# Eight loads ahead of a barrier, and four ScalarE operations made two, in a GRU, experts, state-space and attention kernel

## The chip, the cores and the metric

One core of a Trainium2 chip runs the whole program. The metric is the device time of one execution, in microseconds. PE is the matrix engine (TensorE), PEld its weight loads, DVE the vector engine, ACT the scalar engine, POOL GpSimd, SP the engine that issues the DMAs. PE's granted clock has two levels, 1.2 and 2.4 GHz; a PEclk of 0.5 is the lower and 1.0 the higher.

## The reference, cut to what matters

Four layers act on 4 x 1024 tokens of 128 features, each on the layer-normalised input and each added to the residual: two gated recurrences, eight experts of which each token takes one, a state-space layer with a small network, and a local attention of depth 2. The change touches the seam between the second and third, and one step of the third:

```
yf = einsum('te,etd->td', onehot(top1, E), y_all)          # experts; x = x + yf

u, z  = split(einsum('bld,ed->ble', rmsnorm(x), in_proj_w))
u     = silu(conv(u))
dbc   = einsum('bld,ed->ble', u, x_proj_w)
dt, Bm, Cm = split(dbc, [8, 8 + 16])
dt    = softplus(einsum('blr,dr->bld', dt, dt_proj_w) + dt_proj_b)
s     = s * exp(dt * A) + (dt * u) * Bm                    # 16 states, scanned over time
```

## The kernel before

The token matrix `x` lies transposed in SBUF, features on partitions and the 4096 tokens along the row, and is worked on in eight chunks of 512 tokens (`CH`). Beside it stand `branch`, of the same size, and the constants; both live for the whole program. Each stage is a block with one hand-written program for each engine, and semaphores order the engines. A block ends with a barrier of all engines: each engine drains, POOL gathers them and lets them go; then POOL clears the stage's semaphores, and a second barrier follows.

**Experts** (`experts`, line 514). Tokens are scattered to DRAM by expert, worked on in 40 blocks of 128, and POOL scatters each block's result rows with an indirect DMA into `from_experts` in DRAM (line 739), four to a group. At the end both SP (line 600) and POOL (lines 745, 746) wait for the last of these scatters, `stored[0]` and `stored[1]`. `branch` was written by the recurrences and is not read any more once they are through; the experts do not use it.

**Norm** (`return_and_norm`, line 212). In a new block SP loads the result rows back, a chunk of 256 KB at a time (line 242), into a ring of four buffers `rows`, each again when PE has transposed what was in it (`back`). Behind these eight loads in SP's queue stand eleven loads of the next stage's weights (line 245). PE transposes a chunk (line 259), DVE adds it to `x` (line 303), PE centres it (line 267), ACT squares, PE takes the mean (line 272), ACT computes the two roots (lines 288 to 295), and DVE writes the normalised chunk to `branch` and the root-mean-square one to `x0` (lines 308, 309).

**Time step** (`mamba_and_attention`, line 935). After the convolution come eight chunks `t`, in four blocks of two (`k` = 0, 1). For each block PE computes `dbc` for both chunks (line 1093) into `bank[k]`: rows 0 to 31 are B and C, rows 32 to 39 the low-rank time step, rows 64 to 127 repeat B and C. ACT copies rows 32 to 63 with a bias that makes row 40 a one (line 1240, `dt_low`), then rows 0 to 31 (line 1243, into `rest`), which SP stores to DRAM (line 1029), then all rows as bf16 (line 1244, `parts`), whose lower parts DVE works out (lines 1395 to 1403). PE computes the raw time steps (line 1101) into two banks for a chunk. ACT takes absolute value (line 1251, one for each bank), exponential (line 1254) and logarithm (line 1256), DVE completes the softplus (line 1409). A `matmul` here is issued as two records, so a chunk has four at line 1093 and four at line 1101.

**Scan and attention.** SP broadcasts the stored rows to `b_all` (line 1044), POOL multiplies (line 1348), and 128 steps of the scan follow, with the attention behind them, for the rest of the program. `dt_low` lies in `b_all[32:64, 1:3]`, buffers that the second and third broadcast fill.

## Time and profile before

| | us |
|---|---|
| median of three timed runs (1602.8 to 1604.7) | 1603.2 |
| the profiled execution | 1607.0 |
| its span, from the first to the last instruction | 1605.2 |
| PE, DVE, ACT, POOL busy in the span | 1343, 1208, 1026, 914 |
| from POOL's last scatter of results (its start) to PE's first transpose | 12.2 |
| the norm, from that transpose to DVE's last product | 30.4 |
| ACT's first copy of the time-step stage to POOL's first product of the scan | 43.1 |

The profile is of one execution, so durations and starts are read from it, and a time is compared with the median of the runs. Busy shares are averages over stages with different limits; for a change in one stage the order of time there is read, with what each engine waited for.

### The profile page before, as it was taken

Reading aid. Unit: us, or ns where it says so; the run is one execution under the profiler, and the core shown is the slowest. Engines: PE = TensorE matmul, PEld = TensorE weight load, DVE = VectorE, ACT = ScalarE, POOL = GpSimd, SP = SyncE. Lnnn points to the kernel's source line nnn. Section 1 sums busy time; section 2 is a strip of 40 time slices with the busy share of each in tenths; the row PEclk is TensorE's granted clock in tenths of the full one; section 3 lists DMA queues with packets and bytes.
Section 4 is the critical chain, followed back from the end, with each engine's and each line's share of the span. In section 5 each row is a group of like instructions: output and inputs, shape, how many; then the busy total and the mean of one; then the engine's idle time right before and its main releaser. Section 6 shows DMA issues by size and latency. Waiting matters only on the chain.

```text
span 1605.2 us, 23619 instructions
## 1 busy us (share of the span) xinstructions
PE 1343.4 (84%) x8058; PEld 722.2 (45%) x8058; DVE 1208.1 (75%) x1788; ACT 1025.7 (64%) x1718; POOL 913.9 (57%) x476
## 2 busy tenths in 40 slices
PE   6748199477677888898888889999999999999987
PEld 2315188322223333333333355555555555555552
DVE  2984255267788999999998588888888888888862
ACT  4424055378744554555553588888888888888863
POOL 0343434100298899899895466565555566656540
PEclk9877599787689999999999899999999999999999
DMA  3201221300334433336442112121211111111100
GB/s 114 79 1 32 65 57 48 93 10 7 67 99 100 99 105 92 101 106 170 119 146 63 35 26 47 28 47 28 47 28 43 31 40 34 47 41 34 34 21 27
DMA packets 71038, 96.77 MB, mean 60 GB/s; under 512 B 13651, under 2 KB 32390, under 8 KB 70662
## 3 DMA queue, kind: packets, MB, share of 16 engines
q1 hardware_dynamic: 68614, 90.51, 21.8%
q0 software_dynamic: 2304, 4.74, 0.9%
q8 instruction: 65, 1.06, 0.3%
q14 instruction: 55, 0.45, 0.1%
HBM read 63.73 MB, written 8.41 MB: 45 GB/s over the span
## 4 chain that ended last, share of the span: by engine, by line
PE 46%; ACT 12%; DVE 12%; issue 7%; POOL 2%; DMA 0%; DVEq 0%; SPq 0%; ACTq 0%; POOLq 0%
PE at_two L1766 6%; DVE ssm_state L1445 6%; PE glu_bank L1702 5%; PE ssm_bank L1129 4%; PE at_one L1862 4%; DVE ssm_seen L1454 4%; ACT home_dt L1971 4%; PE glu_bank L1683 4%; PE at_two L1744 3%; PE at_two L1796 3%; PE at_one L1774 3%; PE glu_bank L1728 2%; PE ssm_bank L1163 2%; POOL ssm_dbu L1348 1%; PE ssm_bank L1126 1%
## 5 line engine op out<-in xcount | busy, mean ns | idle before, releaser
L1348 POOL TENSOR_TENSOR ssm_dbu<-ssm_dtu,ssm_b_all 128x1024 f32<-128x1024 f32 x128 | 297.5, 2357 | 31.5 <-DVE home_dt L1409 31.5
L1981 POOL TENSOR_TENSOR at_direct<-at_direct,home_u 128x1024 f32<-128x1024 f32 x64 | 150.9, 2358 | 276.1 <-DVE home_u L2072 276.1
L1274 ACT ACTIVATE ssm_bank<-home_dt,ssm_decay 128x512 f32<-128x512 f32 x256 | 174.6, 690 | 153.1 <-DVE ssm_state L1445 151.7
L1129 PE MATMUL ssm_bank<-ssm_seen,ident 128*128 128x512 f32 x512 | 250.6, 614 | 25.2 <-DVE ssm_seen L1454 23.0
L1129 PEld LDWEIGHTS ssm_bank<-ssm_seen,ident 128*128 128x128 f32 x512 | 97.7, 196 | 146.0 <-issue 86.9
L1445 DVE TENSOR_TENSOR_SCAN ssm_state<-ssm_bank,ssm_carry,ssm_dbu 128x512 f32<-128x512 f32 x128 | 155.8, 1268 | 9.4 <-ACT ssm_bank L1274 9.4
L1445 DVE TENSOR_TENSOR_SCAN ssm_state<-ssm_bank,ssm_dbu 128x512 f32<-128x512 f32 x128 | 147.9, 1206 | 15.3 <-ACT ssm_bank L1274 7.8
L1766 PE MATMUL at_two<-home_u,at_hs 128*128 128x512 f32 x256 | 126.2, 616 | 7.6 <-ACT at_kT L1909 5.5
L1986 POOL TENSOR_TENSOR home_z<-home_z,at_inv 128x1024 f32<-128x1024 f32 x64 | 121.4, 1897 | 18.6 <-DVE at_inv L2083 18.6
L2109 DVE TENSOR_REDUCE at_peak<-at_scores 128x8 f32<-128x1024 f32 x64 | 78.2, 1223 | 61.9 <-PE at_scores L1829 50.6
L1992 POOL TENSOR_TENSOR at_direct<-at_direct,at_rnorm 128x1024 f32<-128x1024 f32 x64 | 121.8, 1903 | 0.2
L1358 POOL TENSOR_TENSOR ssm_seen<-ssm_state,ssm_c_all 128x1024 f32<-128x1024 f32 x40 | 94.1, 2353 | 40.2 <-PE ssm_bank L1129 25.3
L1454 DVE TENSOR_TENSOR ssm_seen<-ssm_state,ssm_bank 128x1024 f32<-128x1024 f32 x88 | 105.5, 1199 | 8.7 <-issue 8.2
L1971 ACT ACTIVATE home_dt<-at_two 128x1024 f32<-128x1024 f32 x64 | 65.4, 1022 | 69.9 <-PE at_two L1796 69.9
L1702 PE MATMUL glu_bank<-home_z 128*128 128x512 f32 (+1 forms) x192 | 91.6, 600 | 1.6 <-DVE home_z L2102 1.2
L2072 DVE TENSOR_TENSOR home_u<-home_dt 128x256 f32<-128x256 f32 x256 | 91.1, 418 | 0.0
L2049 DVE TENSOR_REDUCE at_sums<-home_u 128x16 f32<-128x1024 f32 x64 | 77.4, 1209 | 7.3 <-ACT home_u L1888 7.3
L2079 DVE TENSOR_REDUCE at_total<-home_z 128x8 f32<-128x1024 f32 x64 | 77.6, 1213 | 6.9 <-ACT home_z L1918 6.9
L2065 DVE TENSOR_TENSOR at_direct<-home_dt 128x512 f32<-128x512 f32 x128 | 82.3, 684 | 0.0
L1766 PEld LDWEIGHTS at_two<-home_u,at_hs 128*128 128x128 f32 x256 | 46.6, 193 | 75.3 <-issue 48.9
L2116 DVE TENSOR_TENSOR home_z<-at_scores,at_peak 128x1024 f32<-128x1024 f32 x64 | 78.4, 1224 | 2.2
L1796 PEld LDWEIGHTS at_two<-ident,home_z 128*128 128x128 f32 x512 | 58.4, 140 | 47.5 <-issue 47.5
(247 smaller groups left out, 3100.2 us busy)
## 6 DMA issues: line engine op xcount, KB each, us to landing
ssm_b_all<-ssm_b_rows SPq DMA_DIRECT2D x128, 256.0 KB, 3.4
at_v_mix<-at_v SPq DMA_DIRECT2D x112, 128.0 KB, 2.3
ssm_c_all<-ssm_b_rows SPq DMA_DIRECT2D x40, 256.0 KB, 3.7
at_hs<-branch SPq DMA_DIRECT2D x64, 128.0 KB, 2.4
moe_w<-in_moe_w SPq DMA_DIRECT2D x16, 256.0 KB, 6.0
moe_slot_rows<-moe_to_experts SPq DMA_DIRECT2D x40, 64.5 KB
x<-in_x SPq DMA_DIRECT2D x8, 256.0 KB, 3.7
ssm_norm_rows<-moe_from_experts SPq DMA_DIRECT2D x8, 256.0 KB, 3.2
```

Source lines behind the costliest of these rows:

```text
L1129: last = nc.tensor.matmul(bank[Y0 + half][:], ident[:], seen[:, n % 2, half], start=False, stop=n == STATES - 1)
L1274: nc.scalar.activation(bank[DA0 + half][:], chunk_of(dt[:, half], t), ACT.Exp, scale=decay[:, half, n:n + 1]).then_inc(r[f"da{half}"], 1)
L1348: nc.gpsimd.tensor_tensor(dbu[:, i % RING], dtu[:, t % 2], b_all[:, i % B_RING:i % B_RING + 1, :].broadcast_to([P, 2, CH]), ALU.mult).then ...
L1445: nc.vector.tensor_tensor_scan(state[:, i % RING, half], bank[DA0 + half][:], dbu[:, i % RING, half], start, ALU.mult, ALU.add).then_inc(r ...
L1454: nc.vector.tensor_tensor(seen[:, j % 2], state[:, j % RING], bank[C0][:].unsqueeze(1).broadcast_to([P, 2, CH]), ALU.mult).then_inc(r["see ...
L1702: return nc.tensor.matmul(glu[to][0:size, :], w1[:, c // LAYER_CHUNKS, m * HID + first:m * HID + first + size], normed, start=True, stop=True)
L1766: last = nc.tensor.matmul(two[:, half], at, wqkv[g // PER_LAYER][:, half * INNER:(half + 1) * INNER], start=True, stop=True)
L1796: last = nc.tensor.transpose(two[:, h // 4, (h % 4) * TILE:(h % 4 + 1) * TILE], prob[m % 2][:, h], ident[:])
L1971: nc.scalar.activation(pT[:].rearrange("p h j -> p (h j)"), two[:].rearrange("p a n -> p (a n)"), ACT.Copy).then_inc(s["pT_copied"], 1)
L1981: nc.gpsimd.tensor_tensor(direct[:, n % TURNED], direct[:, n % TURNED], crossed[n % 2], ALU.add).then_inc(s["added"], 1)
L1986: nc.gpsimd.tensor_tensor(prob[m % 2], prob[m % 2], inv[:, m % 2].unsqueeze(2).broadcast_to([P, HEADS, TILE]), ALU.mult).then_inc(s["weigh ...
L1992: nc.gpsimd.tensor_tensor(heads, heads, rnorm[:, n % 2].unsqueeze(2).broadcast_to([P, 2 * HEADS, HEAD]), ALU.mult).then_inc(s["scaled"], 1)
```

## The change

1. `return_and_norm` no longer loads the result rows. SP issues all eight loads at the end of its program in `experts`, right behind its wait for the scatters, and each has a semaphore of its own, `returned[0]` to `returned[7]`, which lives for the whole program. They go into `branch`, chunk by chunk (`returned_rows`), and PE transposes from there. The ring `rows` is gone.
2. POOL's last two waits for the scatters are gone.
3. `dt_low` and the rows of B and C are one copy of rows 0 to 63 into `low`, with a bias of 64 rows (`unit`); SP stores rows 0 to 31 of it. It waits for the store of two chunks before. SP waits for all stores before its second broadcast.
4. The pairs of PSUM banks are one tensor each (`pair`), and the two absolute values of a chunk are one over 1024 elements.

```diff
+def returned_rows(mem, t):
+    return mem["branch"][:, t * CH:(t + 1) * CH].rearrange("p (j d) -> p j d", d=P)
...
 def return_and_norm(...):
-        rows = sb("rows", [P, RING, CH // P, P])
...
         def _(sp):
-            for t in range(CHUNKS_IN):
-                if t >= RING:
-                    sp.wait_ge(back, t - RING + 1)
-                    sp.wait_ge(returned[t % RING], 16 * (t // RING))
-                sp.dma_start(rows[:, t % RING], results[t * CH:(t + 1) * CH].rearrange("(j p) d -> p j d", p=P)
-                             ).then_inc(returned[t % RING], 16)
             for to, of in loads:
                 sp.dma_start(to, of).then_inc(loaded, 16)
             sp.wait_ge(loaded, 16 * len(loads))
-            for n in returned:
-                sp.wait_ge(n, 16 * (CHUNKS_IN // RING))
...
-                    pe.wait_ge(returned[t % RING], 16 * (t // RING + 1))
+                    pe.wait_ge(returned[t], 16)
...
 def experts(...):
             for n in range(2):
                 sp.wait_ge(stored[n], 16 * GROUP * PAIRS)
+            for t in range(2 * SEQS):
+                sp.dma_start(returned_rows(mem, t), from_experts[t * CH:(t + 1) * CH].rearrange("(j p) d -> p j d", p=P)
+                             ).then_inc(mem["returned"][t], 16)
...
                     pool.sem_inc(s["emptied"], 1)
-            for n in range(2):
-                pool.wait_ge(stored[n], 16 * GROUP * PAIRS)
...
 def mamba_and_attention(...):
-        dt_low = b_all[32:64, 1:3]
+        low = b_all[0:64, 1:3]
-        bank = [ring.enter_context(nc.psum_tensor(f"ssm_bank{n}", [P, CH], F32)) for n in range(8)]
+        pair = [ring.enter_context(nc.psum_tensor(f"ssm_bank{n}", [P, 2, CH], F32)) for n in range(4)]
+        bank = [pair[n // 2][:, n % 2] for n in range(8)]
...
-                sp.wait_ge(s["b_low"], done(t))
-                sp.dma_start(b_rows[:, t * CH:(t + 1) * CH], rest[0:2 * STATES, t % 2]).then_inc(b_stored[t % 2], 16)
+                sp.wait_ge(s["low"], done(t))
+                sp.dma_start(b_rows[:, t * CH:(t + 1) * CH], low[0:2 * STATES, t % 2]).then_inc(b_stored[t % 2], 16)
...
                     if i == 1:
                         sp.wait_ge(s["dtraw"], done(2 * SEQS - 1))
+                        for m in b_stored:
+                            sp.wait_ge(m, 16 * (1 + SEQS))
...
-                    pe.wait_ge(s["dt_low"], done(t))
+                    pe.wait_ge(s["low"], done(t))
...
-                                                dt_low[:, k][0:9], start=True, stop=True)
+                                                low[32:41, k], start=True, stop=True)
...
                     act.wait_ge(s["dtraw"], freed(t))
-                    nc.scalar.activation(dt_low[:, k], bank[k][32:64, :], ACT.Identity, bias=unit[32:64]
-                                         ).then_inc(s["dt_low"], 1)
                     act.wait_ge(b_stored[k], b * 16 + 16)
-                    nc.scalar.activation(rest[0:2 * STATES, k], bank[k][0:2 * STATES, :], ACT.Copy).then_inc(s["b_low"], 1)
+                    nc.scalar.activation(low[:, k], bank[k][0:64, :], ACT.Identity, bias=unit[:]).then_inc(s["low"], 1)
...
-                    for half in range(2):
-                        last = nc.scalar.activation(size[:, k, half], bank[2 + 2 * k + half][:], ACT.Abs)
-                    last.then_inc(s["size"], 1)
+                    nc.scalar.activation(size[:, k], pair[1 + k][:], ACT.Abs).then_inc(s["size"], 1)
```

SP at the seam between experts and norm; the exit of the experts' block is line 518 (513 after), the norm's block begins with the branch that waits for `release`. Before:

```order
L597 DMA moe_slot_rows<-moe_to_experts 128x129
L518 UNCONDITIONAL_BRANCH [waits moe_stored1,moe_stored0]
L236 UNCONDITIONAL_BRANCH [waits barrier_Pool_Activation_PE_DVE_SP_release]
L242 DMA ssm_norm_rows<-moe_from_experts 128x4x128 x4
L242 DMA ssm_norm_rows<-moe_from_experts 128x4x128 [waits gru_norm_arrived1,gru_norm_moved]
```

and after:

```order
L591 DMA moe_slot_rows<-moe_to_experts 128x129
L596 DMA branch<-moe_from_experts 128x4x128 [waits moe_stored1,moe_stored0]
L596 DMA branch<-moe_from_experts 128x4x128 x7
L513 UNCONDITIONAL_BRANCH
L239 UNCONDITIONAL_BRANCH [waits barrier_Pool_Activation_PE_DVE_SP_release]
L242 DMA home_dt<-in_in_w 128x512
```

The eight loads moved from behind the barriers to ahead of them, and the weights' loads are now the first behind them.

POOL at the same place; `gather` is its wait for the other engines, the ISA rows are clears of semaphores. Before:

```order
L739 DMA moe_from_experts<-moe_out_rows,moe_owners 9216x128 x3
L518 UNCONDITIONAL_BRANCH [waits moe_stored0,moe_stored1]
L518 ISA [waits barrier_Pool_Activation_PE_DVE_SP_gather]
L218 ISA [waits barrier_Pool_Activation_PE_DVE_SP_gather]
L218 ISA
```

and after:

```order
L736 DMA moe_from_experts<-moe_out_rows,moe_owners 9216x128 x3
L513 UNCONDITIONAL_BRANCH [waits moe_stored0]
L513 ISA [waits barrier_Pool_Activation_PE_DVE_SP_gather]
L223 ISA [waits barrier_Pool_Activation_PE_DVE_SP_gather]
```

The wait for `stored1`, which the last four scatters raise, is gone (the one left is for the group before), and one clear less stands at the norm's exit; one more stands at the end of the program.

ACT in a block of two chunks of the time step, before (the names in the waits are those of semaphores freed by earlier stages):

```order
L1240 ACTIVATE ssm_b_all<-ssm_bank,ssm_unit 32x512 [waits gru_gated_0,gru_fed_0]
L1243 ACTIVATE ssm_dtu<-ssm_bank 32x512 [waits ssm_b_stored0]
L1244 ACTIVATE ssm_parts<-ssm_bank 128x512
L1240 ACTIVATE ssm_b_all<-ssm_bank,ssm_unit 32x512 [waits gru_gated_0,gru_fed_0]
L1243 ACTIVATE ssm_dtu<-ssm_bank 32x512 [waits ssm_b_stored1]
L1244 ACTIVATE ssm_parts<-ssm_bank 128x512
L1251 ACTIVATE ssm_seen<-ssm_bank 128x512 [waits gru_x_done,gru_gated_0]
L1251 ACTIVATE ssm_seen<-ssm_bank 128x512
L1254 ACTIVATE ssm_seen<-ssm_seen 128x1024 [waits gru_gated_1]
L1256 ACTIVATE ssm_seen<-ssm_seen 128x1024 [waits gru_h_0]
```

and after:

```order
L1239 ACTIVATE ssm_b_all<-ssm_bank,ssm_unit 64x512 [waits ssm_b_stored0,gru_off_1,gru_fed_0]
L1240 ACTIVATE ssm_parts<-ssm_bank 128x512
L1239 ACTIVATE ssm_b_all<-ssm_bank,ssm_unit 64x512 [waits ssm_b_stored1,gru_off_1,gru_fed_0]
L1240 ACTIVATE ssm_parts<-ssm_bank 128x512
L1246 ACTIVATE ssm_seen<-ssm_bank 128x1024 [waits gru_h_1,gru_off_1]
L1248 ACTIVATE ssm_seen<-ssm_seen 128x1024 [waits gru_gated_0]
L1250 ACTIVATE ssm_seen<-ssm_seen 128x1024 [waits gru_gated_1]
```

Two instructions a chunk are gone, and the wait for the store stands ahead of the copy that PE's matmuls need.

## Rows read from the trace of the kernel before

**Rows 1.** The page's first row, and the chain that ended last, by engine.
```profile
span 1605.2 us, 23619 instructions
...
PE 46%; ACT 12%; DVE 12%; issue 7%; POOL 2%; DMA 0%; DVEq 0%; SPq 0%; ACTq 0%; POOLq 0%
```

**Rows 2.** Waits of SP, 255 to 345 us: total, times, longest.
```profile
SPq L518 <- PEq L518: 6.1, 1, 6.1
```

**Rows 3.** Line 518: op xcount, ns min/median/max, first and last start.
```profile
L518 POOLq DRAIN  x2: 128/3035/5942, 293.5 to 299.6; - x2
...
L518 PEldq DRAIN  x1: 1187/1187/1187, 284.5 to 284.5; - x1
...
L518 POOLq EVENT_SEMAPHORE_RANGE_CLEAR  x1: 305/305/305, 299.8 to 299.8; - x1
```

**Rows 4.** Timeline, 284 to 304 us: start, length, engine, line, [idle <- releaser].
```profile
284.51 1.16 PE L676 MATMUL moe_bank<-moe_w_now,moe_hidden 128*128 128x128 f32 x8 [0.34 <-ACT moe_hidden L719]
...
291.01 0.96 POOL L739 DMA_INDIRECT moe_from_experts<-moe_out_rows,moe_owners  x1 [0.30 <-issue]
...
300.42 2.04 SPq L242 DMA_DIRECT2D ssm_norm_rows<-moe_from_experts  x4
...
303.22 1.97 PE L259 MATMUL ssm_norm_bank<-ident,ssm_norm_rows 128*128 128x128 f32 x8 [17.55 <-DMA ssm_norm_rows<-moe_from_experts]
```

**Rows 5.** Loads: ssm_norm_rows to landing; SP's timeline; window (us, busy, PEclk, DMA).
```profile
DMA to landing us min/median/max: 2.8/3.2/4.6
...
33.48 11.73 SPq L346 DMA_DIRECT2D moe_w<-in_moe_w  x16
...
304.00:307.00 3.00, 3.00 (x9) 1.53 (x8) 1.38 (x2) 0.00 (x0) 0.00 (x0) 0.50 0.81 238
```

**Rows 6.** Line 1029, the stores of ssm_b_rows.
```profile
DMA to landing us min/median/max: 1.6/1.6/1.6
```

**Rows 7.** Timeline of ACT, 384 to 428 us.
```profile
385.01 0.59 ACT L1243 ACTIVATE ssm_dtu<-ssm_bank 32x512 f32<-32x512 f32 x1
385.50 0.57 ACT L1244 ACTIVATE ssm_parts<-ssm_bank 128x512 bf16<-128x512 f32 x1
386.92 0.68 ACT L1240 ACTIVATE ssm_b_all<-ssm_bank,ssm_unit 32x512 f32<-32x512 f32 x1 [0.85 <-PE ssm_bank L1093]
...
388.83 1.08 ACT L1251 ACTIVATE ssm_seen<-ssm_bank 128x512 f32<-128x512 f32 x2
389.95 1.06 ACT L1254 ACTIVATE ssm_seen<-ssm_seen 128x1024 f32<-128x1024 f32 x1
...
397.53 0.68 ACT L1240 ACTIVATE ssm_b_all<-ssm_bank,ssm_unit 32x512 f32<-32x512 f32 x1 [0.49 <-PE ssm_bank L1093]
...
409.35 1.05 ACT L1251 ACTIVATE ssm_seen<-ssm_bank 128x512 f32<-128x512 f32 x2
```

**Rows 8.** PE, 380 to 428 us: timeline, then groups of instructions.
```profile
401.05 3.70 PE L1093 MATMUL ssm_bank<-home_u,ssm_dbc_w 128*128 128x512 f32 x8
406.61 4.18 PE L1101 MATMUL ssm_bank<-ssm_b_all,ssm_dt_w 9*128 9x512 f32 x8 [1.86 <-ACT ssm_b_all L1240]
410.71 6.65 PE L1093 MATMUL ssm_bank<-home_u,ssm_dbc_w 128*128 128x512 f32 x8
417.29 4.46 PE L1101 MATMUL ssm_bank<-ssm_b_all,ssm_dt_w 9*128 9x512 f32 x8
...
L1093 PE MATMUL ssm_bank<-home_u,ssm_dbc_w 128*128 128x512 f32 x32 | 22.8, 878 | 9.6 <-issue 9.6
L1101 PE MATMUL ssm_bank<-ssm_b_all,ssm_dt_w 9*128 9x512 f32 x32 | 17.0, 675 | 1.9 <-ACT ssm_b_all L1240 1.9
```

**Rows 9.** Windows of the time-step stage: busy time (x), PEclk, DMA share, GB/s.
```profile
380.00:427.00 47.00, 39.38 (x64) 14.52 (x64) 28.11 (x48) 40.67 (x58) 2.35 (x1) 0.72 0.14 31
...
395.30:405.90 10.60, 9.45 (x20) 3.43 (x19) 7.03 (x13) 9.77 (x15) 0.55 (x1) 0.96 0.05 13
```

**Rows 10.** Timeline of POOL, 286 to 428 us.
```profile
427.37 2.35 POOL L1348 TENSOR_TENSOR ssm_dbu<-ssm_dtu,ssm_b_all 128x1024 f32<-128x1024 f32 x1 [31.52 <-DVE home_dt L1409]
```

15 lines of the change are left out of this document (7 added, 8 removed).

## The prediction

> **What bounds the kernel now.** The profiled execution spans 1605.2 us, and its time is 1607.0 us, 1.8 us more for what lies around the span; the median of the timed runs is 1603.2 us. All differences below are made on the profiled execution and taken from the median. I read first the chain that ended last [rows 1]: nearly half of it is PE, and most of the rest ACT and DVE. But the scan and the attention, from POOL's first product at 427.4 [rows 10] to the end, are not touched by the change. So the question is by how much two serial stretches ahead of them, both of them on the way of everything behind, become shorter, and whether the rest simply starts that much earlier.
>
> Next I read what SP waits for at the end of the experts [rows 2], then the exit of that block instruction by instruction [rows 3], then the order of time around it [rows 4]. The reader is to see a gap with no work in it. POOL's last scatter of result rows starts at 291.01 and its record ends 0.96 us later, at 291.97. SP has seen the last scatter landed at 293.3, since it then waits 6.1 us at the exit [rows 2] until 299.6. What holds all engines is POOL: its drain at the block's exit starts at 293.5 and takes 5.94 us [rows 3]. SP's first load starts at 300.42, and PE's first transpose at 303.22 [rows 4]. Last come the eight chunks of the time-step stage (384.3 to 427.4) on ACT and PE [rows 7 to 9].
>
> **Part 1, the loads ahead of the barrier.** Removed: PE's wait for the first load, 303.22 - 300.42 = 2.80 us [rows 4]. The eight loads now lie in SP's program right behind its wait for the scatters, and start at 293.3. The first four took 2.04 us to issue [rows 4], 0.51 each, so eight take 4.1 us and SP is at the exit at 297.4. The nearest row against that is the stretch of 16 loads of the same size issued back to back, 11.73 us or 0.73 each [rows 5], by which SP arrives at 293.3 + 5.9 = 299.2. Both are ahead of 299.4, where POOL's drain ends today. So the issue costs nothing as long as POOL's drain covers it; uncovered it would cost 4.1 to 5.9 us.
>
> The first load lands 2.8 us after its issue [rows 5], at 296.1, before PE is there. The loads moved 238 GB/s at their densest [rows 5], so the 2.1 MB take 8.8 us; with 1.7 us ahead of the first data (2.8 less the 1.1 that one chunk takes at that rate) they are in by 303.8, while PE takes the chunks over some 20 us. No transpose waits.
>
> **Part 2, POOL's two waits removed.** POOL no longer waits for the last scatters before it drains, so it gets there at 291.97 instead of 293.49, 1.52 us sooner. Whether the drain's end moves too depends on what the 5.94 us are, and the trace leaves two readings. On PE the drain of the same exit starts at 284.5, takes 1.19 us, and ends when the last matmuls do (284.51 + 1.16) [rows 3, 4]: a drain there is what the engine has left to do. If POOL's is left-over work of the scatters too, its end at 299.4 stays, and the gain is 0. If the drain itself sets the work off, it ends at 291.97 + 5.94 = 297.9, and the gain is 1.52 us, provided that SP is there. What speaks for the second: scatters follow one another with 0.30 us between them [rows 4], so a scatter leaves POOL free at once. I take 1.5 us and keep 0 for the range; SP at 299.2 would leave 0.2 of it.
>
> The Trainium skill bears on this: its page "Perfetto Trace Analysis" (section "DMA Instruction — SWDGE (GPSIMD)") says that the profiled end of a GpSimd DMA is the end of descriptor generation, not of the transfer. By that rule POOL has nothing of the scatters left at 291.97 but their landing, and the sum would keep the 1.5; by PE's row it would lose them. No row of this trace shows the rule itself at work.
>
> From the drain's end to the first instruction behind the barriers are 300.42 - 299.44 = 0.98 us, unchanged. PE's first transpose thus comes at 297.9 + 1.0 = 298.9 instead of 303.22: **4.3 us**, bounds 2.8 and 4.3. The other 11 loads of the norm stage, which stood behind these eight in SP's queue, start earlier too and nothing waits for them. The engines' work in the norm stage is the same. One of POOL's semaphore clears moves from the norm stage's exit to the end of the program; one such clear is at most 0.3 us [rows 3], once less and once more, 0 in sum.
>
> **Part 3, one copy and one absolute value each.** For each chunk ACT loses the copy of 32 rows. Its own duration is 0.59, but ACT overlaps neighbours: it starts at 385.01 and the next one at 385.50, so it goes with 0.49 us [rows 7]. The remaining copy now writes 64 partitions instead of 32, over the same 512 elements; I take it at the same 0.68, since the copy next to it does 128 partitions in 0.57 [rows 7]. The pair of absolute values starts at 388.83 and the exponential behind it at 389.95, 1.12 us later; one value over 1024 elements takes 1.06 by the nearest row, that exponential [rows 7], and 0.02 to the next. That saves 0.04, up to 0.1 if a read from PSUM is quicker; I take 0.05.
>
> The page "ScalarE: Activation LUTs" of the Trainium skill (section "What ACT_TABLE_LOAD costs") gives 186 ns + 0.833 ns per element and an overlap of 93 ns between neighbours, by which a pair is 1.13 and the single one 1.04, so 0.09 instead of 0.05 each, 0.3 us more over eight chunks; it is an estimate from that page, and the rows decide.
>
> For a block of two chunks that is 2 x (0.49 + 0.05) = 1.08 us, for four blocks 4.3 us. That is the upper bound, since ACT also waits for PE. Block by block:
> First block: ACT's second copy waits 0.85 us for PE's matmuls (at 386.92), so the saved copy only makes that wait longer [rows 7]. Left: 0.1. Second block: the same wait at 397.53, 0.49 us. Left: 0.1. Third block: between 405.87 and the absolute values at 409.35 ACT waits for nothing [rows 7], and PE has the matmuls for it ready in time; all 1.08 count. Fourth block: PE's x8 matmuls from 410.71 took 6.65 us at the half clock, where the same eight take 3.70 at the full one, and the time-step matmuls start only at 417.29 when they are through [rows 8, 9]. With PE as slow as here, ACT is held to about its old place, and the four blocks bring about 0.5 us together; with PE at full clock the fourth brings 1.08 as well, together 2.4. A walk through the stage with these durations, which gives 427.4 for the last time step's end where the trace has 427.0, brings 1.1 us at the clock of the trace. I take **1.2 us**, bounds 0.1 and 3.2.
>
> Added waits: the copy for the time step now also waits for the store of the rows two chunks earlier, and PE's time-step matmuls, ACT's next copy and DVE's chain wait behind it. That store is issued right after its copy, about ten us before, and lands in 1.6 us [rows 6]: 0. SP waits for all stores before its second broadcast; the last one is issued near 418.2 and landed by 420, and SP stands there for PE until 421.8 anyway: 0. If it were late, POOL's first product at 427.37 [rows 10] would be, us for us.
>
> **Sum.** 4.3 + 1.2 = 5.5 us less: 1603.2 - 5.5 = **1597.7 us**.
>
> **The rivals.**
> First, the barrier does not move: POOL's drain ends at 299.4 whenever it is asked for, or SP gets there at 299.2. Then only the load's 2.8 us go, with 1.2: 1599.2 us. PE's drain row speaks for it, the 0.30 us between scatters against it.
> Second, ACT gets all that it saves: PE runs at full clock in all four blocks, and 3.2 to 4.3 us go in place of 1.2. 4.3 + 4.0 = 8.3: 1594.9 us. Only the second block was at 0.96, against 0.72 for the stage as a whole [rows 9].
> Third, SP's exit waits for its own loads. Today no engine reaches a barrier with transfers of its own under way, so the trace cannot exclude it. The exit would come when all eight have landed, at 303.8, and PE's first transpose at 304.8, 1.6 us later than today; with the 1.2 us of part 3 that is 1603.6, and with the 0.1 that part 3 brings where PE bounds it, 1604.7. The point from which this decides is SP's drain in the exit: 7 ns or several us.
> Fourth, the slower side: the clock. Everything moves by some 4 us, and PE idles longer between shorter ACT pieces. PE's matmuls in the stage take 22.8 + 17.0 = 39.8 us at a mean granted clock of 0.72 [rows 8, 9]. A stretch of eight records costs 6.65 - 3.70 = 2.95 us more at the half clock than at the full one, so this decides from two further stretches at half clock (5.9 us against the 5.5 won). With all eight stretches at 6.65 PE has 53.2 us to do, 13.4 more, of which its idle 1.9 us [rows 8] are cover: 11.5 lost against 4.4 won, 1610.3 us. The timed runs lie within 1.9 us of each other, which speaks against such swings. The Trainium skill ("TensorE: Matmul & The Clock Gate", "HAM oscillation — how this bites in real kernels") says that waits between matmuls let the clock fall again; the trace agrees in that it does so inside this stage, and does not say which side of it the change lands on.
>
> **How the numbers follow.** Forecast 0.58; the barrier unmoved 0.20; all of ACT's saving 0.06; SP's exit waits 0.11; the clock 0.05. The range leaves out the second rival's far end, the fourth and the third: low 1603.2 - 4.3 - 3.2 = 1595.7, with half a us for the spread of the runs 1595.2; high 1603.2 - 2.8 - 0.1 = 1600.3, with the same spread and a unit for clock 1601.3. About 0.2% (3.2 us, so 1600.0) is what a measurement can tell from no change. Under it lie the forecast but for its slow tail (0.54), most of the barrier case (0.15) and the second rival (0.06): faster 0.75. Slower takes what the clock case has beyond 1606.4 and little else, 0.03; same 0.22.
>
> **What would show it.** In the profile of the changed kernel: PE's first transpose about 1.0 us behind the end of POOL's drain and without a wait for a DMA (step 1); that drain starting near 292.0 and ending near 297.9 (step 2), or at 299.4 (first rival); SP's drain of a few ns (or of us, third rival); in the time-step stage ACT's waits of 0.85 and 0.49 us longer, not gone, and the stretch from ACT's first copy to POOL's first product 43.1 us before, about 41.9 after. The scan must start 5.5 us earlier and the rest keep its length within 1 us; if it does not, a step is wrong that I have not named.

## The result, and the profile after

The changed kernel took 1599.4 us (median of 11 runs, 1593.2 to 1603.6) beside 1602.8 us for the kernel before (11 runs, 1600.3 to 1604.7) on the same chip: a ratio of 0.9974, 95% interval 0.9963 to 0.9986, which is 4.2 us less (2.2 to 5.9; the two medians alone differ by 3.4). The forecast was 1597.7, or 5.5 us less, in a range from 1595.2 to 1601.3. A second comparison on another chip gave 0.9958 (0.9930 to 0.9985). The runs of the changed kernel spread over 10 us where those of the kernel before spread over 4.4, and that turned out to be the more instructive part of the result.

The profiled execution of the changed kernel is its slowest, 1603.6 us, and its span is 3.4 us below the one of before. The profile page's first row and the chain by engine, to be laid beside [rows 1]:

```profile
span 1601.8 us, 23594 instructions
...
PE 47%; DVE 12%; ACT 11%; issue 7%; POOL 2%; DMA 0%; DVEq 0%; ACTq 0%; SPq 0%; POOLq 0%
```

Its exit from the experts, in the columns of [rows 3]:

```profile
L513 POOLq DRAIN  x2: 134/4800/9467, 287.9 to 298.1; - x2
...
L513 SPq DRAIN  x1: 122/122/122, 297.8 to 297.8; - x1
```

and the order of time around it (start, length, engine, line; [idle before, what ended it]), to be laid beside [rows 4]:

```profile
290.42 0.96 POOL L736 DMA_INDIRECT moe_from_experts<-moe_out_rows,moe_owners  x1 [0.30 <-issue]
292.72 5.01 SPq L596 DMA_DIRECT2D branch<-moe_from_experts  x8
298.87 0.35 SPq L242 DMA_DIRECT2D home_dt<-in_in_w  x1
...
298.92 1.30 PE L254 MATMUL ssm_norm_bank<-ident,branch 128*128 128x128 f32 x5 [13.83 <-PEq L2134]
```

The last scatter's record ends at 290.42 + 0.96 = 291.38. POOL's drain now starts at 287.9, while scatters are still being made (the prediction had it start near 292.0), and takes 9.47 us, so it ends at 297.33: 5.95 us behind the end of the scatter's record. Before, it started at 293.49 and took 5.94 [rows 3]. SP issues its eight loads in 5.01 us and drains at 297.8, in 0.12 us. PE's first transpose comes at 298.92 and waits for no transfer. Measured from the end of the last scatter's record, that transpose came 11.26 us later before (303.22 - 291.97 [rows 4]) and comes 7.54 us later now: 3.7 us won. (The last scatter itself is 0.6 us earlier in this profile, in code that the change doesn't touch.)

Now the time-step stage, the scan and the attention behind it. These are three windows each of the kernel before and of the kernel after; the columns are the stretch, its length, busy time (and instructions) of PE, PEld, DVE, ACT and POOL, then PEclk, DMA share and GB/s:

```profile
384.30:427.40 43.10, 35.81 (x61) 12.87 (x60) 28.15 (x48) 39.25 (x57) 2.38 (x2) 0.74 0.15 34
427.40:870.50 443.10, 370.25 (x845) 150.78 (x845) 410.03 (x371) 227.79 (x401) 403.02 (x174) 0.97 0.41 111
882.00:1567.70 685.70, 650.78 (x5933) 386.91 (x5933) 548.00 (x864) 560.16 (x844) 397.54 (x199) 0.99 0.16 36
```

```profile
380.40:423.20 42.80, 35.41 (x61) 12.86 (x60) 28.14 (x48) 33.99 (x41) 2.37 (x2) 0.74 0.14 34
423.20:864.90 441.70, 367.56 (x845) 149.47 (x845) 409.95 (x371) 227.83 (x401) 403.05 (x174) 0.97 0.41 111
876.40:1563.90 687.50, 652.69 (x5934) 387.41 (x5933) 547.85 (x864) 560.29 (x844) 397.57 (x199) 0.99 0.15 36
```

ACT is 39.25 - 33.99 = 5.3 us less busy in the stage, as the change meant it, and the stage is 0.3 us shorter (43.07 against 42.75 us from ACT's first copy to POOL's first product). Where the saving went is told by what ACT waited for in these 43 us, total, times, longest:

```profile
ACT ssm_b_all L1240 <- PE ssm_bank L1093: 3.9, 3, 2.6
```

```profile
ACT ssm_b_all L1239 <- PE ssm_bank L1091: 6.7, 5, 2.6
ACT ssm_seen L1246 <- PE ssm_bank L1099: 2.8, 4, 0.7
```

3.9 us of waits for PE became 6.7 + 2.8 = 9.5. The instructions themselves save more than was estimated, to be laid beside [rows 7]: the copy of 64 rows lasts 0.68 us but the next one starts 0.59 behind its start, and the absolute value of 1024 elements starts 1.03 to 1.06 ahead of the exponential:

```profile
391.39 0.68 ACT L1239 ACTIVATE ssm_b_all<-ssm_bank,ssm_unit 64x512 f32<-64x512 f32 x1
391.98 0.58 ACT L1240 ACTIVATE ssm_parts<-ssm_bank 128x512 bf16<-128x512 f32 x1
...
409.43 1.01 ACT L1246 ACTIVATE ssm_seen<-ssm_bank 128x1024 f32<-128x1024 f32 x1
410.46 1.06 ACT L1248 ACTIVATE ssm_seen<-ssm_seen 128x1024 f32<-128x1024 f32 x1
```

The scan is 1.4 us shorter and the attention 1.8 us longer, though neither was touched. From PE's first matmul of the stage to the attention's last into `at_two` both profiles have 1187.2 us. So what arrives at the end of this profile is the seam's 3.7 us and the 0.6 ahead of it, less 0.4 in the norm and the convolution and 0.4 behind the attention, and part 3 brings nothing in it.

### The profile page after: what moved, and what is told of

Its sections match the earlier page's. It is cut to its first block, busy times and chain, and to the rows that moved or that the text cites. A ratio compares the mean times of both kernels' runs of the same rounds, so it can differ in the third digit from the quotient of the medians.

```text
span 1601.8 us, 23594 instructions
## 1 busy us (share of the span) xinstructions
PE 1343.0 (84%) x8058; PEld 722.2 (45%) x8058; DVE 1207.8 (75%) x1788; ACT 1020.6 (64%) x1702; POOL 913.9 (57%) x476
## 3 DMA queue, kind: packets, MB, share of 16 engines
q8 instruction: 65, 1.06, 0.3%
## 4 chain that ended last, share of the span: by engine, by line
PE 47%; DVE 12%; ACT 11%; issue 7%; POOL 2%; DMA 0%; DVEq 0%; ACTq 0%; SPq 0%; POOLq 0%
PE at_two L1760 7%; DVE ssm_state L1439 6%; PE glu_bank L1696 5%; PE at_one L1856 4%; PE ssm_bank L1127 4%; DVE ssm_seen L1448 4%; ACT home_dt L1965 4%; PE glu_bank L1677 4%; PE at_two L1738 3%; PE at_two L1790 3%; PE at_one L1768 3%; PE glu_bank L1722 2%; PE ssm_bank L1161 2%; POOL ssm_dbu L1342 1%; PE ssm_bank L1091 1%
```

## The experiments

Twelve runs were made, on three chips. Each stood beside the kernel before on its own chip, and ratios are to that. The kernel before took 1602.2 us on the chip of the first four and 1620.5 and 1621.3 us on the other two, where the profiles show the last scatter some 17 us later (at 306.7 to 308.6 us, in one at 313.9, instead of 289.7 to 292.0); so times of different chips are compared by their ratios only. On the chip of the 1620.5 us the runs of the kernel before themselves spread from 1617.5 to 1628.9, so the spread of a kernel's runs there says little about its clock. The time-step (dt) stage is measured from ACT's first copy to POOL's first product of the scan, the scan from there to the last scan instruction on DVE, the attention from its first to its last matmul into `at_two`.

### The two halves of the change apart

`e1_seam` is the change without its time-step part (parts 1 and 2), `e2_steps` that part alone.

> Parts 1 and 2 alone (loads ahead of the barrier, POOL's two waits gone), the time-step stage as before. In the profile of the full change the time from the end of POOL's last scatter to PE's first transpose was 7.5 us, where the kernel before had 11.3. Theory A (the seam is worth 3.7 us, and part 3 only 0.3): that stretch is 7.5 us here too, and the time is 3.7 us below the kernel before, 1599.1 us. Theory B (the timed runs of the full change spread over 10 us, with a mean granted clock between 0.939 and 0.946, because its time-step stage falls into one of two clock patterns): this kernel, which has the old stage, shows a spread of 4 to 5 us as the kernel before does. Rival (an earlier start of everything behind the seam alone shifts the clock's pattern): its runs spread over 10 us as well, with some near 1595.

Measured: 1599.6 us, ratio 0.9984 (0.9976 to 0.9993), 2.6 us less (1.1 to 3.8), with runs from 1597.3 to 1602.2. From the last scatter's record to PE's first transpose 7.8 us, 0.3 more than in the full change, because SP took longer over its loads:

```profile
291.63 5.30 SPq L596 DMA_DIRECT2D branch<-moe_from_experts  x8
```

The stage took 43.06 us, the scan 443.1 and the attention 685.8, each within 0.1 us of the kernel before (43.07, 443.2, 685.7). The 3.7 us of the seam's path, 3.4 in this profile, lie inside the interval. The spread is that of the kernel before. So the wide spread doesn't come from the seam alone.

> Part 3 alone (one copy of 64 rows, one absolute value of 1024 elements), the seam as before. Prediction's step: ACT's saving is mostly taken by its waits for PE, 1.2 us less, 1601.6 us. By the profile of the full change: 43.07 us became 42.75 from ACT's first copy to POOL's first product of the scan, so 0.3 us less, 1602.5 us. Clock theory: the median falls by 2 us or more and the runs spread over 8 to 10 us, since shorter ACT pieces change where PE waits. PE's first transpose stays 11.3 us behind the end of the last scatter in every case.

Measured: 1603.8 us, ratio 1.0005 (0.9995 to 1.0015): part 3 alone is not faster. But its runs fall into two groups, four of them from 1598.4 to 1599.0 and eight from 1602.1 to 1606.7. The profile is of the first group, 1598.4, and shows a stage that none of the others so far had, 40.9 us with ACT's first copy at 382.1:

```profile
382.10:423.00 40.90, 33.22 (x61) 12.51 (x60) 28.15 (x48) 33.69 (x41) 2.35 (x1) 0.79 0.17 35
```

PE's granted clock is 0.79 there, against 0.74 in the two profiles above, and PE is busy for 33.2 us instead of 35.4. The attention took 684.7 us. Neither 0.3 nor 1.2 us was right, then: part 3 alone brings some 3.5 us in four executions and costs some 2 in the other eight. The mean granted clock of each run splits them in the same way: 0.942 to 0.944 in the four, 0.937 to 0.940 in the eight, 0.938 to 0.941 in the runs of the kernel before. What the slower group does, 2 us above the kernel before, no profile caught, and it stays open.

### Two patterns of the clock in the same kernel

`e8_after_again` is the full change once more, unchanged.

> The full change once more, beside the others. Its timed runs lay in two groups, near 1595.4 and near 1600.5. Pattern theory: the profile shows the time-step stage either at 42.75 us with 441.7 and 687.5 us for scan and attention, or at 40.9 with 442.5 and 684.7, nothing in between, and the time is 3.8 us lower in the second; the runs fall into the two groups again. Rival (the spread comes from somewhere ahead of the seam, which varied by 2 us between profiles): the stage stays at 42.75 in any profile and the groups are not seen again.

Measured: ratio 0.9958 (0.9930 to 0.9985), runs of 1611.1 to 1622.9. Its profile fell into the other pattern:

```profile
395.70:436.60 40.90, 33.23 (x61) 12.43 (x60) 28.14 (x48) 33.73 (x41) 2.37 (x2) 0.79 0.17 35
436.60:879.10 442.50, 367.92 (x845) 149.83 (x845) 409.94 (x371) 227.77 (x401) 403.09 (x174) 0.97 0.41 111
890.60:1575.20 684.60, 649.75 (x5933) 386.46 (x5933) 548.03 (x864) 559.94 (x844) 397.56 (x199) 0.99 0.16 36
```

The same program, the same instructions in the same order: 40.91 us instead of 42.75 for the stage, 442.6 for the scan instead of 441.7, 684.6 for the attention instead of 687.5. From ACT's first copy to the attention's last matmuls that is 1179.5 us against 1183.5, 3.9 us less when nothing is rounded. The kernel before needs 1183.4 for it. So the new steps are worth 0.0 us in the first pattern and 3.9 in the second. With the seam's 3.7 the two should give 1599.1 and 1595.2, and the eleven timed runs of the first comparison lie near these: five from 1593.2 to 1596.8, with mean granted clocks of 0.945 and 0.946, five from 1599.4 to 1601.0, with 0.940 to 0.942, and the profiled one at 1603.6, with 0.939. The two lengths of the stage, and nothing between, are what the pattern theory expected. The groups of the repetition's runs are not so clean: two lie at 1611.1 and 1611.8, three from 1615.0 to 1615.4, one at 1622.9, and the profiled one is among the three, at 1615.1, although it has the short stage, where the theory wants the lower group. Its last stretch, behind the attention's last matmul into `at_two`, is 38.0 us, as long as in the first pair of profiles (37.5 and 37.9) and 1.9 to 3.2 more than in the other eleven. So at least one more stretch has two lengths, and the time of a run alone doesn't tell the pattern of the stage.

The attention's part of the difference goes with the clock as well. Added up from the clock records of the traces, the attention has 10.2 us at the half clock where it takes 684.2 to 684.7 us (seven profiles), 13.7 where it takes 685.7 or 685.8 (before, e1 and e10), and 17.1 where it takes 687.5 to 687.9 (after, e4, e6 and e7), though no instruction in it was changed.

Where they part is seen in PE's timeline in the last two of the four blocks. First the profile of the change, then that of its repetition:

```profile
398.54 5.83 PE L1091 MATMUL ssm_bank<-home_u,ssm_dbc_w 128*128 128x512 f32 x8
...
407.93 3.70 PE L1091 MATMUL ssm_bank<-home_u,ssm_dbc_w 128*128 128x512 f32 x8
```

```profile
412.40 3.70 PE L1091 MATMUL ssm_bank<-home_u,ssm_dbc_w 128*128 128x512 f32 x8
...
421.41 5.27 PE L1091 MATMUL ssm_bank<-home_u,ssm_dbc_w 128*128 128x512 f32 x8
```

These are the same eight records of the third and of the fourth block. In the first profile the half clock falls on the third block, 5.83 us instead of 3.70, and the time-step matmuls of that block come late for ACT. In the second it falls on part of the fourth (5.27), where ACT has work in front of it.

What goes with it lies 80 us ahead, at the start of the norm, where PE comes from idling at the half clock. The windows ahead of and behind the moment at which the clock rose, in the first profile and in the repetition:

```profile
298.90:303.90 5.00, 4.98 (x15) 3.47 (x16) 1.53 (x3) 1.86 (x2) 0.00 (x0) 0.50 1.12 329
303.90:307.00 3.10, 3.10 (x11) 1.53 (x10) 0.53 (x1) 1.96 (x4) 0.00 (x0) 1.00 0.15 21
```

```profile
315.20:318.80 3.60, 3.60 (x10) 2.27 (x11) 1.38 (x2) 1.25 (x1) 0.00 (x0) 0.50 1.07 305
318.80:322.00 3.20, 3.20 (x15) 1.88 (x14) 0.69 (x1) 1.97 (x4) 0.00 (x0) 1.00 0.61 175
```

PE's first transpose is at 298.92 in the one and 315.20 in the other, so the clock rose 5.0 us behind it and 3.6 us behind it. Over all profiles of kernels that have no filler work and do all of the reference's work:

| kernel | clock rose, behind first transpose | transpose to next stage's PE | clock fell, ahead of dt stage's PE | dt stage | scan | attention |
|---|---|---|---|---|---|---|
| before (old steps) | 4.2 | 33.1 | 4.8 | 43.1 | 443.2 | 685.7 |
| e1 (old steps) | 3.9 | 32.7 | 4.8 | 43.1 | 443.1 | 685.8 |
| after | 5.0 | 33.2 | 4.5 | 42.8 | 441.7 | 687.5 |
| e4 | 4.8 | 33.2 | 4.5 | 42.8 | 441.8 | 687.5 |
| e6 (norm altered; from its first matmul there) | 3.8 | 32.3 | 4.6 | 42.7 | 441.8 | 687.9 |
| e2 | 4.3 | 33.1 | 4.7 | 41.0 | 442.5 | 684.7 |
| e3 | 3.6 | 32.6 | 4.8 | 40.9 | 442.5 | 684.7 |
| e8 | 3.6 | 32.6 | 4.8 | 40.9 | 442.6 | 684.6 |
| e12 | 3.1 | 32.3 | 4.9 | 40.9 | 442.5 | 684.7 |

With the new steps there are two outcomes and nothing between: a fall of the clock 4.7 us or more ahead of the stage's first matmul goes with the short stage, 4.6 or less with the long one. The rise alone doesn't sort them: e6 has 3.8 and the long stage, e2 4.3 and the short one. Which of them an execution gets goes with tenths of a us at this fall. That the fall decides is a correlation over seven profiles; `e12_queues_waits`, below, is the one that was forecast from it.

### What sets the barrier

`e3_pool_waits` is the full change with POOL's waits kept:

```
+            for n in range(2):
+                pool.wait_ge(stored[n], 16 * GROUP * PAIRS)
```

> The full change with POOL's two waits for the last scatters kept (parts 1 and 3). If POOL's drain has 5.95 us of its own that start when it is reached or when the last scatter's record has ended, whichever is later, it starts about 1.5 us behind the last scatter's end and ends 7.5 us behind it, SP has issued its loads by then, and PE's first transpose is 8.4 us behind the scatter's end: 0.9 us more than in the full change, which SP's issue held. Rival (the drain's end is the end of left-over work of the scatters, so the waits cost nothing): 7.5 us, as in the full change.

The exit of the experts and PE's first transposes (the last scatter's row starts at 288.78 and lasts 0.95):

```profile
L513 POOLq DRAIN  x2: 128/3035/5942, 291.3 to 297.4; - x2
...
L513 SPq DRAIN  x1: 122/122/122, 296.4 to 296.4; - x1
```

```profile
298.21 1.30 PE L254 MATMUL ssm_norm_bank<-ident,branch 128*128 128x128 f32 x5 [14.77 <-PEq L2136]
```

POOL's drain starts 1.5 us behind the scatter's record, takes 5.94 us and ends 7.5 us behind it, and SP is there 0.7 us before. PE's first transpose comes 8.5 us behind the record, as expected. So the drain has 5.94 us of its own which begin when both the engine has nothing left and the drain is asked for. Part 2 of the prediction is confirmed in its mechanism. The time was not as that alone would have it: 1596.0 us (1594.4 to 1596.4), ratio 0.9961 (0.9949 to 0.9974), 6.2 us below the kernel before, where the full change was 4.2 below. The norm starts 0.9 us later, and the profile is of the clock's second pattern (table): 3.7 - 0.9 + 3.9 = 6.7 us is what the two make by the path.

`e4_two_queues` gives four of the eight loads to ACT:

```
-            for t in range(2 * SEQS):
+            for t in range(0, 2 * SEQS, 2):
...
+            for n in range(2):
+                act.wait_ge(stored[n], 16 * GROUP * PAIRS)
+            for t in range(1, 2 * SEQS, 2):
+                act.dma_start(returned_rows(mem, t), from_experts[t * CH:(t + 1) * CH].rearrange("(j p) d -> p j d", p=P)
+                              ).then_inc(mem["returned"][t], 16)
```

> The full change with the eight loads issued by two engines, four by SP and four by ACT, which is idle there. In the full change SP's eight issues took 5.0 us and its drain came 0.5 us behind the end of POOL's. If SP was the last one at the barrier, PE's first transpose now comes 0.97 us behind the end of POOL's drain, about 7.0 us behind the last scatter's end instead of 7.5, and the time is 0.4 to 0.5 us below the full change. Rival (the transfers under way slow the barrier itself, or POOL's drain takes longer beside the issue): 7.5 us as before.

```profile
289.39 0.96 POOL L741 DMA_INDIRECT moe_from_experts<-moe_out_rows,moe_owners  x1 [0.30 <-issue]
291.69 2.03 SPq L596 DMA_DIRECT2D branch<-moe_from_experts  x4
291.71 2.13 ACTq L722 DMA_DIRECT2D branch<-moe_from_experts  x4
...
297.33 1.94 PE L254 MATMUL ssm_norm_bank<-ident,branch 128*128 128x128 f32 x8 [13.28 <-PEq L2139]
```

The last scatter's record ends at 290.35 and POOL's drain at 296.31, 5.96 us behind it. SP and ACT are through with their issue by 293.84. PE's first transpose is 6.98 us behind the scatter's record, where the full change had 7.54. So in the full change SP's issue was the last at the barrier, by 0.6 us. The time is 1599.4 us, ratio 0.9983 (0.9974 to 0.9992), no better than the full change: its profile is of the first pattern, and so, by their spread of 3.3 us and their mean granted clocks of 0.938 to 0.942, may all its runs be.

`e12_queues_waits` joins the two: loads by two engines, POOL's waits kept.

> Loads by two engines, and POOL's two waits for the last scatters kept. POOL's drain alone sets the barrier: PE's first transpose 8.4 us behind the end of the last scatter, 1.4 later than with two queues and no waits. Pattern theory: in ten profiles the new stage took 40.9 us wherever the granted clock rose within 4.3 us of PE's first transpose in the norm (or the norm began so that the next fall came 4.7 us or more ahead of the stage), and 42.7 where it rose 4.8 to 5.0 us behind it; a later start puts it into the first group. Then this kernel is 2 us or more faster than the one without the waits, though its norm starts 1.4 us later. Rival (a later start is a loss as such): 1.4 us slower than the kernel of the two queues.

```profile
L513 POOLq DRAIN  x2: 128/3035/5942, 308.7 to 314.8; - x2
...
L513 SPq DRAIN  x1: 122/122/122, 310.6 to 310.6; - x1
```

```profile
395.70:436.60 40.90, 33.22 (x61) 12.36 (x60) 28.14 (x48) 33.78 (x41) 2.38 (x2) 0.79 0.17 35
```

PE's first transpose came 8.5 us behind the last scatter's record and the stage took 40.85 us, both as expected from the pattern theory. Ratio 0.9967 (0.9955 to 0.9979) where e4 had 0.9983 (0.9974 to 0.9992) on another chip: 2.6 us better, with intervals that overlap a little, although its norm starts 1.5 us later. The profiles say it more plainly: from PE's first matmul of the stage to the attention's end 1183.3 us against 1187.3. A later start went with a shorter path behind it, which a sum of path lengths can't give.

`e6_early` has PE transpose and DVE add the first chunk in the experts' block, while POOL drains:

```
+            pe.wait_ge(mem["returned"][0], 16)
+            for j in range(CH // P):
+                last = nc.tensor.transpose(bank[0][:, j * P:(j + 1) * P], returned_rows(mem, 0)[:, j], ident[:])
+            last.then_inc(s["home"], 1)
...
+            dve.wait_ge(s["home"], 1)
+            nc.vector.tensor_tensor(x[:, 0:CH], x[:, 0:CH], bank[0][:], ALU.add)
```

> The full change, and the first returned chunk is transposed by PE and added by DVE at the end of the experts, ahead of the barrier, which POOL's drain holds for 6 us; the norm begins with the centring matmul of that chunk. If the barrier doesn't move (DVE is done about 297.3 in the times of the profile of the full change, where POOL's drain ends at 297.4) the norm's chain is 1.9 us shorter at its start, and the matmul of the convolution stage starts 1.9 us earlier against the end of the last scatter, 38.9 us instead of 40.8. Rival (the norm is bound further on by ACT and DVE, or the barrier is later): no gain at that point. The total may differ from this by the clock pattern of the time-step stage, 4 us one way or the other.

```profile
309.96 5.85 SPq L599 DMA_DIRECT2D branch<-moe_from_experts  x8
```

```profile
314.01 0.69 DVE L888 TENSOR_TENSOR x<-x,moe_bank 128x512 f32<-128x512 f32 x1 [10.90 <-PE moe_bank L682]
```

A miss. DVE was through at 314.7, near POOL's drain's end at 314.6, but SP took 5.85 us for its loads and held the barrier until 316.0. The convolution's first matmul came 40.7 us behind the last scatter's record, where the full change has 40.8 and 40.5 in its two profiles. From PE's first matmul of the norm to it there were 32.3 us instead of 33.2 and 32.6, so of the 1.9 us at the head of the norm 0.3 to 0.9 reached its end. Ratio 0.9964 (0.9940 to 0.9988).

### What bounds the time-step stage

`e7_no_abs` leaves out the absolute value: the exponential reads the raw time step, so its time steps are not the reference's.

```
-                    nc.scalar.activation(size[:, k], pair[1 + k][:], ACT.Abs).then_inc(s["size"], 1)
-                    act.wait_ge(s["size"], done(t))
-                    nc.scalar.activation(size[:, k], size[:, k], ACT.Exp, scale=-1.0).then_inc(s["small"], 1)
+                    nc.scalar.activation(size[:, k], pair[1 + k][:], ACT.Exp, scale=-1.0).then_inc(s["small"], 1)
```

> The full change without the absolute value: ACT takes the exponential of the raw time step straight from the banks, so the time steps are not those of the reference; ACT has eight instructions of 1.02 us less in the stage. If ACT bounded the stage it would be 8.2 us shorter, about 34.6 us. If PE at its granted clock bounds three of four blocks, as the waits of the profile say, it is 2 to 3 us shorter only, 38 to 41 us, with ACT's waits for PE longer by the rest. If the clock falls further because PE's own stretches come with more waiting, it is not shorter at all.

```profile
396.50:431.80 35.30, 31.39 (x61) 11.67 (x60) 27.98 (x48) 25.64 (x33) 2.35 (x1) 0.84 0.18 38
```

```profile
ACT ssm_b_all L1239 <- PE ssm_bank L1091: 6.9, 6, 2.6
ACT ssm_seen L1246 <- PE ssm_bank L1099: 3.7, 5, 0.7
```

This fell between the theories. The stage took 35.3 us, 7.4 less than the long pattern and 5.6 less than the short one, of 8.1 us taken from ACT; ACT still waits 6.9 + 3.7 = 10.6 us for PE. PE is at a clock of 0.84 where it had 0.74 and 0.79, and its own 35.4 and 33.2 busy us became 31.4. Up to 409 us its timeline is that of the short pattern, to 0.1 us in each stretch. There, in the repetition, PE pauses for 1.60 us ahead of the third block's time-step matmuls (417.70) and the clock falls at 421.2; here it makes no pause and the clock holds until its matmuls end at 427.7. That fits ACT's work costing time partly through the pauses that it forces on PE. But pauses are not all of it. PE is busy without a pause from 392.70, and the clock falls at 401.4 all the same, in the time-step matmuls, which read nine rows:

```profile
398.92 4.78 PE L1099 MATMUL ssm_bank<-ssm_b_all,ssm_dt_w 9*128 9x512 f32 x8
```

```profile
398.00:401.40 3.40, 3.40 (x9) 1.38 (x8) 3.03 (x6) 1.63 (x3) 0.00 (x0) 1.00 0.15 39
401.40:408.20 6.80, 6.80 (x9) 2.31 (x8) 3.69 (x6) 4.45 (x6) 2.35 (x1) 0.50 0.00 0
```

The two falls in the first three blocks of the changed kernel's first profile, at 385.8 and 396.0, come with PE busy since 376.64 as well. Whether it is the nine rows was not tried. Ratio 0.9932 (0.9905 to 0.9959).

`e5_warm` takes the clock's fall ahead of the stage away, with work whose results are not used:

```
+            pe.wait_ge(s["z"], done(2 * SEQS - 2))
+            for n in range(4):
+                nc.tensor.matmul(bank[0][:], ident[:], x0[:, cols(n)], start=True, stop=True)
             pe.wait_ge(s["z"], done(2 * SEQS - 1))
+            for n in range(5):
+                nc.tensor.matmul(bank[W1][:], ident[:], x0[:, cols(n)], start=True, stop=True)
             pe.wait_ge(s["u"], done(2 * SEQS - 1))
```

> The full change with nine filler matmuls on PE in its idle time ahead of the time-step stage (their results are not used): four behind the last but one gate of the convolution, five behind the last. In all kernels so far PE was idle for 9.6 us there, its granted clock fell, and the stage began at the half clock; its length was 42.75 us at one pattern of clocks (22.3 us of it at the half clock) and 40.9 at the other (17.0 us). Clock theory (the stage is bound by PE at the half clock, and which stretches are slow decides what the one copy and the one absolute value bring): the stage begins at the full clock, PE's first eight records take 3.7 us instead of 6.5, and the stage is at least 4 us shorter, under 39 us; the time falls to 1595 or less. Rival (ACT bounds the stage): no more than 1 us shorter. A third way: the clock falls later inside the stage all the same, since PE waits for ACT there, and the stage stays at 41 to 43 us.

PE's timeline at the start of the stage, to be held against 6.52 us for the same eight records in the profile of the change, and the stage's window:

```profile
391.87 3.70 PE L1096 MATMUL ssm_bank<-home_u,ssm_dbc_w 128*128 128x512 f32 x8
...
408.16 5.25 PE L1096 MATMUL ssm_bank<-home_u,ssm_dbc_w 128*128 128x512 f32 x8
```

```profile
393.90:432.30 38.40, 31.63 (x61) 11.77 (x59) 28.14 (x48) 33.56 (x41) 2.38 (x2) 0.82 0.14 38
```

The first records take 3.70 us, PE's lead over ACT's first copy falls from 3.8 to 2.0 us, and the stage is 38.4 us, 4.4 or 2.5 less than the two patterns. So the clock theory holds in size for the stage; the third way holds too, since from the third block on there is half clock again (408.16, 5.25 us). Ratio 0.9935 (0.9911 to 0.9959); on the same chip the full change had 0.9958, medians 1612.0 and 1615.0 us, with intervals that overlap. From PE's first matmul of the stage to the attention's end it is 1179.6 us, against 1183.3 and 1187.2 in the two profiles of the full change.

`e11_warm_old` has the fillers with the old steps, to price part 3 with a faster PE.

> Parts 1 and 2 of the change and the nine fillers, with the old time-step stage (two copies, two absolute values). With the fillers the new stage took 38.4 us. If the fillers take PE off the path, ACT's whole saving (4.3 us by the prediction's durations) shows now: this kernel's stage takes 42 to 43 us, and part 3 is worth about 4 us with a fast PE. Rival (what the fillers gave was independent of ACT's work, part 3 worth about nothing in every case): 38.4 to 39 us. PE's first records take 3.7 us in every case.

`e9_warm_queues` is e5 with the loads by two engines.

> The kernel of the two queues with the nine filler matmuls ahead of the time-step stage. If the two gains are in different places they add: PE's first transpose 7.0 us behind the end of the last scatter, the stage from ACT's first copy to POOL's first product about 38.4 us, as with the fillers alone, and PE's first matmul of the stage 2.0 us ahead of ACT's first copy instead of 3.8. Against the kernel before: 0.5 (queues) and 10 (change and fillers) us less. Rival (the shift of the seam throws the stage into another pattern of clocks): the stage at 40 us or more.

Both ran on one chip. PE's first transpose of e9 came 7.0 us behind the last scatter's record, as expected. Their stage windows, e11's first:

```profile
395.70:437.90 42.20, 35.20 (x61) 12.55 (x60) 28.14 (x48) 39.23 (x57) 2.38 (x2) 0.75 0.16 34
```

```profile
399.60:441.30 41.70, 35.19 (x61) 12.65 (x59) 28.15 (x48) 33.82 (x41) 2.35 (x2) 0.75 0.14 35
```

By time, e11 has 0.9955 (0.9943 to 0.9968) and e9 0.9936 (0.9923 to 0.9949), medians 1614.2 and 1610.4. That is 3.7 us (3.1 by the ratios), of which 0.9 are the two queues' by these profiles (7.87 and 6.98 us from the scatter's record to the first transpose); so with fillers part 3 is worth 2 to 3 us, with intervals that overlap. e11's stage is as long as was expected, 42.15 us and 3.8 above e5's, but the profiles show that it isn't simply ACT's saving becoming visible: both have PEclk 0.75, and the stages are 42.15 and 41.70 us, 0.45 apart, and e9's profile missed the 38.4 us that was expected. A stage of the same code took 38.4 in e5 and 41.7 here.

`e10_fillers` adds fillers at two more places, at the end of PE's program in the experts and behind the time-step stage.

```
+            for n in range(11):
+                nc.tensor.matmul(bank[0][:], centre[:], x[:, 0:CH], start=True, stop=True)
...
+            for n in range(5):
+                nc.tensor.matmul(bank[W1][:], ident[:], x[:, cols(n)], start=True, stop=True)
             pe.wait_ge(s["parts"], done(2 * SEQS - 1))
```

> The same with filler matmuls at two more places where PE sat idle and its clock fell: eleven at the end of the experts (12 us idle), five behind the time-step stage (5.7 us idle). Clock theory: the norm stage, which ran 9.3 of its 33.2 us at the half clock, is 1 to 2 us shorter, and the scan, which had 24 to 30 us at the half clock near its start and took 441.7 to 443.2 us, is 1 to 2 us shorter. Rival (ACT and DVE bound both): neither moves by more than 0.5 us, since a faster PE only waits longer there, or the scan is later by the fillers in its way.

```profile
393.00:431.40 38.40, 36.79 (x67) 14.06 (x66) 28.14 (x48) 33.56 (x41) 2.37 (x2) 0.82 0.18 38
313.70:346.50 32.80, 20.67 (x64) 9.98 (x64) 16.12 (x28) 23.40 (x34) 0.00 (x0) 0.88 0.24 66
```

The norm took 32.8 us (32.3 to 33.4 elsewhere). But it is a weak trial: the norm began at the full clock and fell to the half one 1.2 us later, and in all it had 7.7 us at the half clock instead of 9.3. The scan took 443.2 us with 23.9 us at the half clock, where e5 has 30.3 and the same 443.2: there the clock's 6.4 us bought nothing, as the rival says. For the norm the question stays open. The stage took 38.4 us once more. Ratio 0.9941 (0.9927 to 0.9954), the same as e9 and e5 within their intervals. Of the kernels that do all of the work, those with fillers ahead of the stage have the lowest ratios, 0.9935 to 0.9955. How much better than the change as it was made is less sure: 3 us by the medians on the one chip where both ran.

## Why the prediction was right, point by point

**Removed load (2.80 us).** Right: PE's first transpose waits for no transfer, and the loads issued ahead of the barrier cost the barrier little. SP's drain took 0.12 us with its own loads under way, so the third rival is out.

**POOL's drain.** Right in mechanism and in size: its end moved from 7.47 to 5.95 us behind the last scatter's record, 1.52 us, and e3 gave it back. The prediction chose this over PE's row by the 0.30 us between scatters. The rule of the Trainium skill ("Perfetto Trace Analysis", "DMA Instruction — SWDGE (GPSIMD)"), by which a GpSimd DMA's record ends with descriptor generation, is borne out: SP's wait for the landing ended only 1.3 us behind the record (292.72 against 291.38), and the drain's 5.94 us were the same with the transfers landed and with them under way. It doesn't say what those 5.94 us are, and no run here does.

**SP's issue.** The mis-sized term of the seam. Taken at 4.1 us, from four issues in 2.04, it measured 4.6 to 5.9 in eight profiles; the row of 16 loads in 11.73 us, named as the other bound (5.9 us for eight), was the better one, the mean being 5.3. As POOL's drain now ended 1.5 us earlier against the last scatter, SP became the last at the barrier by 0.6 us. Hence 3.7 us from the seam instead of 4.3. The prediction held "covered until 299.4" against the drain's old end first and drew the case of the new one only as a side remark.

**Part 3.** The step that failed. What ACT sheds was taken too small. From the start of the copies to that of the bf16 copy it is 1.20 us before and 0.59 now, 0.61 less a chunk where 0.49 was taken, since the copy that stays overlaps its neighbour and the prediction took its whole 0.68; the pair of absolute values went from 1.10 to 1.05 on average, as taken. Over eight chunks that is 5.3 us, what ACT's busy time fell by, where the prediction had 4.3 as its upper bound. The first and second block went as forecast: ACT's waits of 0.85 and 0.49 us are now 1.61 and 1.25. The third, of which all 1.08 us were counted, did not: PE took 5.83 us for its eight records where the trace before had 3.70, and ACT waited 0.36, 0.89 and 0.74 us for PE. The taken 1.2 us rested on walking the stage with the clock of the one trace, block by block. With the new steps the half clock fell on other blocks: 0.3 us in one pattern and 2.2 in the other within the stage, and with what the scan and the attention then did 0.0 and 3.9 us. 1.2 us is none of the values that occur.

**The rest keeps its length within 1 us.** Wrong: the scan -1.4 and the attention +1.8 us in the profile of the change. The last stretch, behind the attention's last `at_two` matmul, was 34.8 to 36.1 us in eleven profiles and 37.5 to 38.0 in three (before, after, e8). Those three have 7.5 to 7.7 us of it at the half clock, the others 1.6 to 5.8; what sets that wasn't tried.

**The clock as a rival.** It was priced as a loss of 11.5 us at a chance of 0.05, and it is in fact what part 3 lives on, in both directions. The Trainium skill ("TensorE: Matmul & The Clock Gate", "HAM oscillation — how this bites in real kernels") says that waits between matmuls bring the clock down again; e5 and e7, with less waiting, agree at 0.82 and 0.84 for the stage against 0.74, but e7's fall at 401.4 us came with no wait ahead of it. That the timed runs of the kernel before lay within 1.9 us of each other was no evidence for the changed one: the old steps showed one pattern in both profiles, the new ones two, and even the kernel before spread over 11 us on another chip. That the 5.5 us of the forecast lie close to the measured 4.2 is therefore partly luck: 3.7 and 7.6, the values of the two groups, lie on either side.

## What to carry to other kernels

At a block's end, look at which engine drains last and how long, and count what every engine issues ahead of it: work put under a long drain is free only until the drain is shortened too. In a stage where PE is at the half clock for half of the time (22.3 of 42.8 us here), the value of a shorter ACT instruction can't be read from one trace: profile the changed kernel more than once, look for two lengths of the same stage, and time enough runs to see groups. If PE idles ahead of such a stage, matmuls without use in that idle time are a cheap trial.

## What the runs showed of the hardware

POOL's drain behind indirect DMAs took 5.94 to 5.96 us from the later of its own start and the end of the last record, in every profile, with the transfers landed or not. PE's, ACT's and DVE's ended with their last instruction (0.05 us behind it, when they had issued no DMA). An engine's drain didn't wait for transfers that the engine had issued (SP and ACT, 0.12 and 0.15 us). Eight loads of 256 KB each took one queue 4.6 to 5.9 us to issue; two queues took 2.0 and 2.1 us for four each, side by side. And one program with one order of instructions has stages of two lengths, 40.9 and 42.8 us, which go with 17.0 and 22.3 us at the half clock; its attention has 684.6 and 687.5 us, with 10.2 and 17.1. The granted clock also fell with PE busy for 8.7 us without a pause, in matmuls of nine rows (e7, 401.4 us). In the scan 6.4 us less at the half clock changed nothing (443.2 us both in e10 and in e5).
